# Normalization sums of five batches moved to VectorE inside the eigenvector recurrence of a graph kernel

## The reference

```python
h = relu(layernorm(x))                      # x: (128, 120, 1024)
U = eigh(D^-1/2 (diag(deg) - A) D^-1/2)     # A: (120, 120); all eigenvectors
agg = einsum('vn,bvd->bnd', U, h)
o = relu(agg @ W1 + b1) @ W2 + b2           # 1024 -> 128 -> 1024
# theta, phi, g: products of o over the 120 nodes; phi and g max-pooled by 2
y = softmax(theta^T phi) g                  # per batch, 1024 x 512
z = batchnorm(wo y) + o
out = x + einsum('nv,bvd->bnd', U, z) + z
```

## Time and profile before

| | us |
|---|---|
| median of 3 runs | 3321.01 (3320.54 to 3321.21) |
| the profiled execution, its own time | 3320.95 |
| its span in the profile | 3319.2 |
| PE busy in the span | 3169.2 (95%) |
| ACT busy | 2407.8 (73%) |
| DVE busy | 2316.4 (70%) |
| POOL busy | 1884.4 (57%) |

### The profile page before, as it was taken

One profiled execution on the slowest core, in us unless ns is written; L12 is line 12 of the kernel. 1 busy time (PEld: TensorE's weight loads), 2 busy tenths in 40 slices (PEclk: granted clock), 3 DMA queues, 4 the chain that ended last, 5 costly groups with the idle time before them and its releaser, 6 DMA issues.

```text
span 3319.2 us, 65434 instructions
## 1 busy us (share of the span) xinstructions
PE 3169.2 (95%) x16040; PEld 2544.0 (77%) x16040; DVE 2316.4 (70%) x6363; ACT 2407.8 (73%) x4380; POOL 1884.4 (57%) x1722
## 2 busy tenths in 40 slices
PE   6888987799999999999999999999999999999997
PEld 4677776577777777777777777777777777777775
DVE  8998888766666666666666666666666666666664
ACT  6889999666666666666666666666666666666665
POOL 3222212166666666666666666666666666666665
PEclk9999999899999999999999999999999999999998
DMA  3333444222222222222222222222222222222222
GB/s 101 92 101 108 111 113 113 61 61 72 72 72 72 72 72 72 72 72 72 72 72 72 72 72 72 72 72 72 72 73 72 74 72 72 72 72 72 72 72 66
DMA packets 111582, 256.28 MB, mean 77 GB/s; under 512 B 47500, under 2 KB 49797, under 8 KB 111493
## 3 DMA queue, kind: packets, MB, share of 16 engines
q1 hardware_dynamic: 111493, 255.25, 27.7%
HBM read 190.69 MB, written 63.44 MB: 77 GB/s over the span
## 4 chain that ended last, share of the span: by engine, by line
PE 81%; DVE 10%; ACT 5%; issue 4%; POOL 0%; DMA 0%; DVEq 0%; POOLq 0%; ACTq 0%; SPq 0%
PE ps_M L811 8%; PE ps_M L813 8%; PE ps_M L812 8%; PE ps_S L888 7%; PE ps_E L811 7%; PE ps_O L811 7%; PE ps_E L812 7%; PE ps_O L813 7%; PE ps_O L812 7%; PE ps_E L813 7%; PE ps_M L872 3%; ACT P L544 2%; ACT P L534 1%; ACT fT L551 1%; PE ps_S L893 1%
## 5 line engine op out<-in xcount | busy, mean ns | idle before, releaser
L508 POOL TENSOR_TENSOR p_lo<-p,p_hi 128x512 fp32r<-128x512 f32 x1024 | 1374.9, 1343 | 942.1 <-ACT p_hi L663 938.1
L658 ACT ACTIVATE p<-ps_E 128x512 f32<-128x512 f32 x1024 | 614.1, 600 | 331.9 <-PE ps_E L813 307.3
L1423 DVE TENSOR_REDUCE nmx<-ps_S 128x1 f32<-128x512 f32 x1024 | 658.8, 685 | 130.7 <-PE ps_S L888 126.7
L663 ACT ACTIVATE p_hi<-p 128x512 fp32r<-128x512 f32 x1024 | 647.1, 632 | 32.6
L811 PE MATMUL ps_E<-o_hi,Q_hi 123*128 123x512 f32 x1024 | 426.9, 417 | 0.0
L811 PE MATMUL ps_O<-p_hi,v_hi 128*121 128x512 f32 x1024 | 406.2, 397 | 4.1 <-POOL p_lo L508 4.1
L813 PE MATMUL ps_O<-p_lo,v_hi 128*121 128x512 f32 x1024 | 406.3, 397 | 0.0
L812 PE MATMUL ps_E<-o_hi,Q_lo 123*128 123x512 f32 x1024 | 404.7, 395 | 0.0
L812 PE MATMUL ps_O<-p_hi,v_lo 128*121 128x512 f32 x1024 | 404.5, 395 | 0.0
L813 PE MATMUL ps_E<-o_lo,Q_hi 123*128 123x512 f32 x1024 | 403.7, 394 | 0.0
L1403 DVE TENSOR_REDUCE gf<-ps_M 128x256 f32<-128x512 f32 x256 | 177.1, 692 | 262.7 <-PE ps_M L813 262.7
(11 more groups left out here) (364 smaller groups left out, 5953.2 us busy)
## 6 DMA issues: line engine op xcount, KB each, us to landing
rbc<-r_dram SPq DMA_DIRECT2D x128, 484.0 KB
xin<-in_x_dram SPq DMA_DIRECT2D x128, 480.0 KB, 4.1
xt<-in_x_dram SPq DMA_DIRECT2D x128, 480.0 KB, 4.9
out_dram<-y SPq DMA_DIRECT2D x128, 480.0 KB, 3.7
o_hi<-mrow SPq DMA_DIRECT2D x256, 2.0 KB
dcol<-y SPq DMA_DIRECT2D x128, 4.0 KB, 2.0
r_dram<-rcol SPq DMA_DIRECT2D x128, 4.0 KB, 1.4
W1s<-in_L_gnn_W_dram SPq DMA_DIRECT2D x1, 512.0 KB, 4.1
```

Of the source, the lines that this page charges most:

```text
L508: pool.tensor_tensor(p_lo[:, c % 4, :], p[:, c % 4, :], p_hi[:, c % 4, :].bitcast(F32), ALU.subtract).then_inc(plo_sb, 1)
L658: act.activation(p[:, c % 4, :], ps_E[c % 2][:, :], ACT.Exp).then_inc(p_sb, 1)
L663: act.activation(p_hi[:, c % 4, :], p[:, c % 4, :], ACT.Copy).then_inc(phi_sb, 1)
L1423: dve.tensor_reduce(nmx[:, c:c + 1], ps_S[SBANK[c]][:, :], AX.X, ALU.max, negate=True).then_inc(max_sb, 1)
```

## The change

1. Batches 100, 103, 107, 110 and 115 (`BY_DVE`) get their mean and their sum of squares on DVE: two `bn_stats` of 512 elements, one `bn_aggr`, and two `tensor_scalar` on one column that write `lnd` (the negated mean) and `rstd`. ACT leaves out `b_sum` and `b_sq` of these batches; `b_relu` of such a batch waits for `stat_done`.
2. The DVE pieces stand inside `minors` and `count`: `spare` keeps a counter, and where the counter has reached 22 times the number of batches done it puts one of the four pieces there, the next one at the next `spare`, and so on. The first piece, for batch 100, stands at step 1 of the grid round; the five batches' pieces begin at step 1 and step 42 of the grid round, at step 18 of the second round, in the `count` of the second round, and at step 30 of the third.
3. These batches are loaded into two spare stretches of `P1`, by SP: the first two (100 and 103) right behind the load of batch 95, the other three right behind later loads (batch 107 behind the load of batch 104, which waits for the square of batch 101). The other batches use `xin` by their own count.
4. `GRID_AT` is 98 in place of 102.
5. The splits of W2 and theta stand in front of DVE's wait for PE's transpose of `Z`.

```diff
@@ sync
+            def load_stat(n):
+                before = [m for m in range(n) if STAT_IN[m] == STAT_IN[n]]
+                if before:
+                    sp.wait_ge(relu_done, BY_DVE[before[-1]] + 1)
+                s = BY_DVE[n]
+                sp.dma_start(xdv[STAT_IN[n]], x[s:s + 1, :, :].rearrange("a n d -> n (a d)")).then_inc(xd_in[STAT_IN[n]], 16)
+            def load_late(a):
+                sp.wait_ge(sq_done, a - 1)
...
             load(0, 0)
             load(1, 1)
-            rounds(sp, 2, B, load)
+            rounds(sp, 2, UNROLL, load)
+            load_stat(0)
+            load_stat(1)
+            for a in range(UNROLL, len(BY_ACT)):
+                load_late(a)
+                for n in range(2, len(BY_DVE)):
+                    if BY_ACT[a - 2] == BY_DVE[n] - STAT_AHEAD:
+                        load_stat(n)
@@ scalar, slot(k)
                 if k < B:
-                    b_relu(k, par)
-                if k < B - 1:
-                    b_sq(k, par)
+                    b_relu(k)
+                if k < B - 1 and k not in BY_DVE:
+                    b_sq(k)
...
-                if k + 1 < B:
-                    act.wait_ge(sq_done, k + 1)
-                    b_sum(k + 1, 1 - par)
+                if k + 1 < B and k + 1 not in BY_DVE:
+                    b_sum(k + 1)
@@ vector
+            def stats():
+                n, i = stats_done[0], stat_part[0]
+                s, b = BY_DVE[n], STAT_IN[n]
+                if i == 0:
+                    dve.wait_ge(xd_in[b], len([m for m in range(n + 1) if STAT_IN[m] == b]) * 16)
+                if i < 2:
+                    mark(dve.bn_stats(bst[:, i * 6:i * 6 + 6], xdv[b][:, i * 512:i * 512 + 512]))
+                    stat_part.append(last())
+                elif i == 2:
+                    need(stat_part[-1])
+                    mark(dve.bn_aggr(bag[:, :], bst[:, :]))
+                    stat_part.append(last())
+                else:
+                    need(stat_part[-1])
+                    if n >= 2:
+                        dve.wait_ge(relu_done, BY_DVE[n - 2] + 1)
+                    mark(TS(lnd[:, n % 2, :], c_(bag, 0), -1.0, None, ALU.mult))
+                    TS(rstd[0:N, s:s + 1], c_(bag, 1), float(D), None, ALU.mult).then_inc(stat_done, 1)
+                    stats_done[0] += 1
+                stat_part[0] = (i + 1) % 4
+            def spare(us):
+                clock[0] += us
+                if stats_done[0] < len(BY_DVE) and (stat_part[0] or clock[0] >= stats_done[0] * STAT_EVERY):
+                    clock[0] += (0.5, 0.5, 0.1, 0.15)[stat_part[0]]
+                    stats()
@@ minors, each step, between T(SM) and T(SP)
+                    spare(0.5)
                     need(turned)
@@ count, behind the signs
+                spare(3.0)
@@ behind count of each later round
+                spare(3.2)
@@ behind the last use of the basis' vectors
-            dve.wait_ge(pe_out, 5)
-            dve.tensor_copy(VT[:, :], ps_up[0:N, 0:N]).then_inc(dve_out, 1)
-            i_hi = did(dve.tensor_copy(W2hi[:, :], W2f[:, :]))
+            split(W2hi[:, :], W2lo[:, :], W2f[:, :])
+            split(Qwhi[:, :], Qwlo[:, :], wn[:, 0, :])
+            dve.wait_ge(pe_out, 5)
+            dve.tensor_copy(VT[:, :], ps_up[0:N, 0:N]).then_inc(dve_out, 1)
...
-GRID_AT = 102
+GRID_AT = 98
+BY_DVE, STAT_IN = (100, 103, 107, 110, 115), (0, 1, 0, 1, 0)
+UNROLL, STAT_AHEAD, STAT_EVERY = 96, 6, 22.0
```

More of the change, by code:

```diff
@@ L93, in build @@
             lns = eb("lns", [N, 2, 1])
+            lnd = eb("lnd", [N, 2, 1])
+            bst = eb("bst", [N, 12])
+            bag = eb("bag", [N, 2])
+            xdv = [P1[0:N, b * H:(b + 8) * H] for b in (B - 12, B - 20)]
             QA = eb("QA", [N, 2 * N])
@@ L228, in build @@
         x_in = [sem(f"x_in{i}") for i in range(2)]
+        xd_in = [sem(f"xd_in{i}") for i in range(2)]
+        stat_done = sem("stat_done")
         mean_done = sem("mean_done")
@@ L337, in load @@
                 sp.dma_start(xin[:, par, :], x[bass.ds(k, 1), :, :].rearrange("a n d -> n (a d)")).then_inc(x_in[par], 16)
+            def load_stat(n):
[6 more added lines that the diff above has]
+                sp.wait_ge(sq_done, a - 1)
+                s = BY_ACT[a]
+                sp.dma_start(xin[:, a % 2, :], x[s:s + 1, :, :].rearrange("a n d -> n (a d)")).then_inc(x_in[a % 2], 16)
             load(0, 0)
             load(1, 1)
-            rounds(sp, 2, B, load)
+            rounds(sp, 2, UNROLL, load)
[6 more added lines that the diff above has]
+                        load_stat(n)
             sp.wait_ge(filled, 1)
@@ L477, in rstds @@
             def rstds(a, z):
-                pool.wait_ge(sq_done, z)
+                pool.wait_ge(sq_done, by_act(z))
+                late(pool, stat_done, by_dve(z))
                 chain(pool.tensor_scalar(rstd[0:N, a:z], rstd[0:N, a:z], 1.0 / D, LN_EPS, ALU.mult, ALU.add))
@@ L531, in _, with b_sum, b_relu, b_sq @@
         def _(act):
[L532 to L538, removed]
-                late(act, tr_done, s - 1)
[L540 to L544, removed]
+            def b_sum(s):
+                a = by_act(s)
+                late(act, sq_done, a)
+                act.wait_ge(x_in[a % 2], (a // 2 + 1) * 16)
+                act.activation(junkx, xin[:, a % 2, :], ACT.Copy, scale=-1.0 / D,
+                               accum_out=lns[:, a % 2, 0:1]).then_inc(mean_done, 1)
+            def b_relu(s):
+                a, n = by_act(s), by_dve(s)
+                late(act, tr_done, s - 1)
+                if s in BY_DVE:
+                    act.wait_ge(stat_done, n + 1)
+                    act.activation(frelu[:, s % 2, :], xdv[STAT_IN[n]], ACT.Relu, bias=lnd[:, n % 2, 0:1]).then_inc(relu_done, 1)
+                else:
+                    act.wait_ge(mean_done, a + 1)
+                    act.activation(frelu[:, s % 2, :], xin[:, a % 2, :], ACT.Relu, bias=lns[:, a % 2, 0:1]).then_inc(relu_done, 1)
+            def b_sq(s):
+                a = by_act(s)
+                act.wait_ge(mean_done, a + 1)
+                act.activation(junkx, xin[:, a % 2, :], ACT.Square, bias=lns[:, a % 2, 0:1],
                                accum_out=rstd[0:N, s:s + 1]).then_inc(sq_done, 1)
@@ L556, in b_p1 @@
                 if s == B - 4:
-                    act.wait_ge(sq_done, B)
+                    act.wait_ge(sq_done, by_act(B))
                 act.activation(P1[0:N, s * H:(s + 1) * H], ps_m[par][0:N, 0:H], ACT.Copy).then_inc(p1_done, 1)
@@ L576, in _ @@
             act.wait_ge(consts, 1)
-            b_sum(0, 0)
+            b_sum(0)
             def keep(*copies):
@@ L1111, in need @@
                 dve.wait_ge(dve_step, i)
+            clock, stats_done, stat_part = [0.0], [0], [0]
+            def stats():
[10 more added lines that the diff above has]
+                    stat_part.append(last())
+                else:
+                    need(stat_part[-1])
[10 more added lines that the diff above has]
+                    stats()
             def minors():
@@ L1270, in _ @@
                    PW[:, :, :, :, 1].rearrange("p i g e -> p i (g e)"), ALU.add))
+            assert stats_done[0] == len(BY_DVE)
             step(TS(PD, PS[:, 0:SEG, :, :], TINY, None, ALU.add))
@@ L1360, in _ @@
             T(Cop[0:N, 2 * H + 1:OPS], ps_up[0:N, N:2 * N], ident[0:N, 0:N], ALU.add).then_inc(dve_out, 1)
-            need(i_hi)
-            mark(T(W2lo[:, :], W2f[:, :], W2hi[:, :].bitcast(F32), ALU.subtract))
-            split(Qwhi[:, :], Qwlo[:, :], wn[:, 0, :])
             dve.wait_ge(dve_out, 9)
@@ L1443, with by_dve, by_act @@
 LN_RATE, LN_LEAD, LN_BEHIND = (9, 1), 2, 3
-GRID_AT = 102
+GRID_AT = 98
 WY_SLOT, WY_STEPS = 94, 19
 WY_T, WY_G = 1, 3
+BY_DVE, STAT_IN = (100, 103, 107, 110, 115), (0, 1, 0, 1, 0)
+UNROLL, STAT_AHEAD, STAT_EVERY = 96, 6, 22.0
+BY_ACT = [s for s in range(B) if s not in BY_DVE]
+def by_dve(s):
+    return len([t for t in BY_DVE if t < s])
+def by_act(s):
+    return s - by_dve(s)
 WY_P = lambda level: 3 + 2 * level
```

## The result

The changed kernel takes 3351.9 us, median of 4 runs (3350.34 to 3352.44), against 3321.11 us for the kernel before beside it: a ratio of 1.0092, 95% interval 1.0079 to 1.0105. It is 30.8 us slower. The forecast was 3351.5, with a chance of 0.93 for slower. One of the ten executions of the run with the early first loads took 9869 us; its ratio leaves that one out, its median does not.

The account below looks back on a forecast made before the run. ACT sets the pace, DVE within 0.7 us. Parts: +32.4 at relu(100), +8.1 at relu(110), +0.7 factor in slot 100, -9.8 sums and squares, -0.8 tail: +30.6 on 3320.95, 3351.5 us; range 3342 to 3361.

Parts of the forecast that it names:

- transpose to first product, less than before: At the first part's end, DVE takes up `Cop` at once because the W2 and theta splits moved: 0.8 us saved.
- The order of issue: On SP's queue, batch 100's load is issued behind batch 95's, which waits for batch 93's square; it lands at about 475.4.
- The price of a batch on DVE: One batch's two `bn_stats`, aggregation and one-column operations in front of the recurrence: 1.5 us (0.9 to 2.7).
- PE's restart at half clock: Behind PE's wait at the grid's count, the first batch runs at half rate: 2.8 us more than at full clock.
- The rival of a long half clock: PE stays at half rate up to relu(110), each further batch costing 2 us: +3 to +6, 3354 to 3358; chance 0.10.
- the third wait: ACT at relu(110) waits 8.1 us for the fourth batch's sums from DVE, with all later slots queued behind.
- the second wait: DVE at step 18 of the second round waits 7.3 us for batch 107's load, held behind the square of 101.
- slot 100: ACT's slot for batch 100, without a square but with 0.7 us waiting for PE's factor step: 4.1 us.
- The rival without waits: Transfers arrive in time from DVE's first piece on, so the change does what it says: -7.3 us, 3313.7; chance 0.05.
- first wait: DVE at step 1 of the grid round waits 25.8 us for batch 100's load, the whole recurrence queued behind.

Follow-up runs that it names:

- the run with the early first loads: Changed kernel with the loads of batches 100 and 103 issued behind that of batch 87 instead of 95; 3323.17 us against 3320.21, ratio 1.0008.
- the run with batch 107 earlier: Changed kernel with batch 107 loaded as soon as relu(100) frees its place, the wait for batch 100 kept; 3344.18 us against 3320.21, ratio 1.0070.
- the run at 102: Changed kernel with the grid's count back at batch 102, loads unchanged; 3343.04 us against 3319.43, ratio 1.0070.
- the run without waits: Changed kernel with loads of 100 and 103 behind 87, 107 behind relu(100), later pieces at 45, 60, 82; 3313.18 us (3312.07 with count at 99).

## Why the prediction was right

All of its steps can be laid beside the trace of the changed kernel. One thing has to be known first: in that execution ACT is 1.4 us later from the tenth batch on than in the profiled execution of before, and DVE's Householder steps 1.5 to 1.6, because of PE's clock in the first 47 us (last section). It is no effect of the change: the kernel before with nothing but the count moved has it too (1.5), and the changed kernel with the early first loads has 0.2. The measured times of day below contain it; the forecast ones do not.

| step | forecast | measured |
|---|---|---|
| DVE waits for batch 100 | 25.8 | 26.14 |
| grid's count written | 524.2 | 525.43 |
| PE waits for it | 31 | 30.3 |
| relu(100) starts | 530.9 | 531.89 |
| DVE waits for batch 107 | 7.3 | 6.95 |
| ACT waits before relu(110) | 8.1 | 8.94 |
| relu(110) starts | 578.9 | 580.39 |
| `Z` done on DVE | 652.0 | 652.45 |
| transpose of `Z` on PE | 658.5 | 659.93 |
| transpose to first product, less than before | 0.8 | 0.76 |

- **The order of issue** was the step that decided, and it held: the load of batch 100 was issued at 471.46 and landed 5.82 us later, the one behind it 7.5 us after its own issue. One load alone took 4.2; each load ahead on the queue added about 1.7, near the 1.75 us that its packets take. The Trainium skill (DMA: Bandwidth & Descriptors, Anatomy of one DMA) states its fit of 2.0 us plus the bytes at 436 GB/s for transfers issued from GpSimd, which the prediction does not say; for a load of 0.49 MB with another one right ahead of it that makes at most 4.3 us, an estimate. Here SP issues, and 5.8 was measured. The early loads took the wait away and all but 3 of the 31 us.
- **The price of a batch on DVE** was put somewhat too high, and this hid in the sum. The groups by line:

```profile
L1156 DVE BATCH_NORM_STATS2 bst<-P 120x6 f32<-120x512 f32 x10 | 6.9, 689 | 33.2 <-DMA P<-in_x_dram 33.1
L1160 DVE BATCH_NORM_AGGREGATE bag<-bst 120x2 f32<-120x12 f32 x5 | 1.0, 201 | 0.0
L1166 DVE TENSOR_SCALAR lnd<-bag 120x1 f32<-120x1 f32 x5 | 0.7, 145 | 0.0
L1167 DVE TENSOR_SCALAR rstd<-bag 120x1 f32<-120x1 f32 x5 | 0.7, 141 | 0.0
```

  A `bn_stats` of 512 elements takes 0.689 us, for 0.68 from the two reductions. From the first `bn_stats` at 477.30 to the count at 525.43 it is 48.13 us, against 45.75 for the same stretch before (449.60 to 495.35): 1.19 us a batch where I had 1.5. Behind the grid the same instructions of DVE, laid beside those of before, move from 22.0 us late at batch 107's first piece to 26.0 at `Z`: 1.3 us for each of the three batches. From start to start the pieces of batch 100 take 1.45 us in front of the recurrence's steps (0.61, 0.60, 0.12 and 0.12), so the rest of the difference is idle time of the recurrence that they fill.
- **PE's restart at half clock.** The windows of the changed kernel, in and behind the stall:

```profile
508.50:525.90 17.40, 0.41 (x2) 0.41 (x3) 16.24 (x33) 0.00 (x0) 0.00 (x0) 0.50 0.00 0
525.90:534.00 8.10, 8.10 (x51) 8.10 (x52) 7.39 (x52) 2.37 (x5) 0.94 (x3) 0.65 0.01 3
534.00:540.00 6.00, 4.90 (x44) 4.54 (x44) 3.39 (x27) 6.00 (x15) 0.79 (x3) 1.00 0.19 42
```

  The 16 products behind the stall took 3.62 us, 0.23 each as at the kernel's beginning, and the next 16 took 1.91 (timeline of PE). One batch at half rate, as forecast; the rule of the Trainium skill (TensorE: Matmul & The Clock Gate, What's actually happening) that an idle TensorE falls to 1.2 GHz and busy work brings 2.4 back agrees with this trace. The rival of a long half clock did not come: behind 534 PE is back. The forecast overlooked that the third wait does the same: PE stands still for 7.8 us in front of its transposes at 582.61, and behind that the clock is down once more:

```profile
579.50:586.00 6.50, 3.40 (x17) 3.43 (x18) 6.19 (x50) 5.61 (x11) 1.36 (x1) 0.50 0.01 1
```

  This cost nothing that shows: ACT, which sets the pace there, does not wait for PE again before its last product.
- **Each wait handed on.** The experiments separated what the sum only claimed: that 6.7 of the 8.9 us of the third wait are the second one's (the run with batch 107 earlier), and that PE's stall at the count costs nothing beyond DVE's lateness, but for the second wait, which it brings about (the run at 102).
- **Errors that cancelled.** That most of these places are met within half a microsecond is in part luck. Two loads in a row took longer than forecast: 6.4 us from the first one's issue at 470.92 to the second's landing at 477.28, and 6.7 from 537.77 to 544.42, where the forecast had 5.9. Against that, the two batches before the count cost DVE 0.6 us less, and slot 100 took 3.58 us for 4.1: of the 0.7 us added there for a factor step of PE hardly any came. The upper end of the range adds up to 3359.3, not 3359.5; nothing hangs on it.
- **The rival without waits** was priced at 3313.7. Built, it came out at 3313.18 and 3312.07. It needed three corrections, not one: first loads, second load, and the order in which DVE makes the sums. The price had only the first two, the transfers; with the sums in their old order ACT would still have waited for those of batch 110, some 3 us by the run with the early first loads (8.6 less 5.6 of DVE's wait, an estimate; it was not run). So its closeness is luck too.

## What to carry to other kernels

When an engine takes over work inside a serial chain, ask first when the queue that feeds it may issue the load, by the semaphore in front of it, and not only what the work costs: here 1.2 to 1.3 us of work a batch cost 26 us at its first wait. Long waits of about the same length on several engines can be one delay; move the place where it shows (the count at 102) and see whether the end moves. A freed resource is a gain only if every later hand-over comes in time, so list what each consumer asks for and when, and set the producer's order by that.

## What the runs showed of the hardware that was not expected

- The same instructions at the kernel's beginning take different times from one execution to the next: relu(10) starts 0.5 us earlier up to 3.1 us later than in the profiled execution of before, in runs whose code up to there is the same. It goes with PE's clock. The first record of the granted clock in a trace, at its full level, stands at 40.6 us in the earliest run, at 41.6 in before, at 46.9 in the changed kernel, and at 52.7 in the run at 102, the latest. In the changed kernel 6 products at 42.63 took 1.64 us, against 0.92 for 6 at 42.15 in before: PE stays at half rate some 5 us longer. (The windows view gives 1.00 ahead of the first record, so the half rate there, in the earlier trace rows too, is read from the products alone.) A difference of 1 to 2 us between two profiled executions is therefore not the kernels' until the offset of a batch ahead of the change is taken off.
- Two loads issued ahead of another one hold that one up: ACT waited 1.1 us for the load of batch 96 in the changed kernel, and 1.5 us at the corresponding place in the run without waits. The forecast had not counted this; in the changed kernel it lay inside the wait for the count.
- Where ACT works without a wait and without a factor step, its slot is 4.32 us in the changed kernel against 4.29 before: 0.8 us over batches 84 to 95 and 116 to 127. In slots with a factor step there is no such difference. Its cause stays open.
